# In the sync queue of a convolution and neighbourhood attention kernel, the queries' fill of a chunk goes behind the collecting of denominators and the first maxima, the keys' fill ahead of the spreads

## The reference

```python
x = x + _L0_conv_ref(_gn(x), L0_conv_W)        # 3x3 convolution, 32 groups of 4 channels
x = x + _L1_conv_ref(_gn(x), w_qkv, b_qkv, rpb, w_proj, b_proj)
```

## Time and profile before

| | us |
|---|---|
| median of 3 runs | 1148.31 |
| lowest and highest | 1146.44, 1153.41 |
| the profiled execution | 1146.23 |
| its span, first to last instruction | 1144.3 |
| TensorE (PE) busy | 1023.5 (89%) |
| VectorE (DVE) busy | 800.6 (70%) |
| ScalarE (ACT) busy | 661.2 (58%) |
| GpSimd (POOL) busy | 377.5 (33%) |
| mean granted TensorE clock | 0.916 |

### The profile page before, as it was taken

One profiled execution on the slowest core, in us unless ns is written; L12 is line 12 of the kernel. 1 busy time (PEld: TensorE's weight loads), 2 busy tenths in 40 slices (PEclk: granted clock), 3 DMA queues, 4 the chain that ended last, 5 costly groups with the idle time before them and its releaser, 6 DMA issues.

```text
span 1144.3 us, 41255 instructions
## 1 busy us (share of the span) xinstructions
PE 1023.5 (89%) x16485; PEld 702.3 (61%) x16485; DVE 800.6 (70%) x2159; ACT 661.2 (58%) x1840; POOL 377.5 (33%) x759
## 2 busy tenths in 40 slices
PE   5999999997898989898999898898999898989883
PEld 3666665555566666665666666666666666666661
DVE  3477856336778687776877786868686777777770
ACT  2111312106686767676776768586767776777561
POOL 5000104014252516161534344352525151625230
PEclk9999999998899899988998999899798888998895
DMA  9320014406675757484857676665757584857621
GB/s 248 98 85 30 30 43 124 105 29 175 142 165 131 177 135 188 110 211 98 199 126 197 144 178 139 171 162 136 169 130 183 125 197 102 210 106 178 120 57 58
DMA packets 141525, 154.72 MB, mean 135 GB/s; under 512 B 31344, under 2 KB 119824, under 8 KB 141080
## 3 DMA queue, kind: packets, MB, share of 16 engines
q1 hardware_dynamic: 140344, 148.20, 54.3%
q0 software_dynamic: 992, 3.90, 1.1%
HBM read 84.05 MB, written 67.60 MB: 133 GB/s over the span
## 4 chain that ended last, share of the span: by engine, by line
PE 72%; issue 9%; DMA 7%; DVE 7%; SPq 3%; POOL 1%; ACT 0%; POOLq 0%; DVEq 0%
PE PS L1298 16%; PE PS L1365 14%; PE PS L1402 11%; PE PS L1386 7%; PE PS L1310 6%; PE PS L1379 5%; PE PS L1347 5%; PE PS L1412 4%; DMA area<-q_parts 4%; DVE S L1148 2%; DMA area<-x 2%; PE PS L1327 2%; DVE area L1127 1%; DVE masked L1159 1%; PE PS L1425 1%
## 5 line engine op out<-in xcount | busy, mean ns | idle before, releaser
L690 POOL TENSOR_TENSOR late<-masked 128x48 f32<-128x48 f32 (+1 forms) x512 | 151.5, 296 | 525.2 <-DVE masked L1159 506.0
L1148 DVE TENSOR_TENSOR S<-PS,bias 128x384 f32<-128x384 f32 (+1 forms) x512 | 282.7, 552 | 6.6 <-PE PS L1365 5.1
L1365 PE MATMUL PS<-area 97*128 97x48 bf16 (+1 forms) x4096 | 258.2, 211 | 31.6 <-issue 12.2
L880 ACT ACTIVATE S<-S 128x384 f32<-128x384 f32 (+1 forms) x512 | 272.0, 544 | 9.8 <-DVE S L1148 7.7
L1138 DVE TENSOR_REDUCE mcol<-PS 128x6 bf16<-128x480 f32 (+2 forms) x288 | 176.1, 611 | 127.5 <-PE PS L1386 127.5
L873 ACT ACTIVATE VT<-PS 128x128 f32<-128x128 f32 x448 | 127.8, 285 | 230.3 <-PE PS L1347 229.8
L1365 PEld LDWEIGHTS PS<-area 97*128 97x128 bf16 x4096 | 185.8, 105 | 80.1 <-DVE S L1148 17.5
L1402 PE MATMUL PS<-S,VT 128*18 128x48 f32 x8192 | 203.9, 219 | 28.6 <-issue 24.6
L1402 PEld LDWEIGHTS PS<-S,VT 128*18 128x18 f32 x8192 | 121.3, 101 | 171.4 <-issue 100.4
L1298 PE MATMUL PS<-padded,wconv 128*128 128x392 f32 x576 | 204.4, 503 | 0.0
L1159 DVE TENSOR_TENSOR masked<-PS,cst 128x96 f32<-128x96 f32 (+1 forms) x512 | 128.6, 251 | 65.2 <-PE PS L1402 64.4
(11 more groups left out here) (85 smaller groups left out, 865.0 us busy)
## 6 DMA issues: line engine op xcount, KB each, us to landing
area<-k_parts SPq DMA_DIRECT2D x32, 1008.0 KB, 9.1
area<-q_parts SPq DMA_DIRECT2D x64, 294.0 KB, 10.3
k_parts<-area SPq DMA_DIRECT2D x32, 504.0 KB, 5.9
q_parts<-area SPq DMA_DIRECT2D x64, 196.0 KB, 3.8
k_parts<-area SPq DMA_DIRECT2D x32, 336.0 KB, 5.2
late<-x_mid SPq DMA_DIRECT2D x18, 392.0 KB, 4.8
out<-area SPq DMA_DIRECT2D x18, 392.0 KB
den<-sums SPq DMA_DIRECT2D x132, 49.0 KB
```

Source lines behind the costliest of these rows:

```text
L690: nc.gpsimd.tensor_tensor(sel[:, c % SEL_RING, :, :, t0:t0 + count], m[:, :, 0], m[:, :, 1], ALU.add).then_inc(s["summed"], 1)
L880: nc.scalar.activation(S[:, n % 4, 0:cols], S[:, n % 4, 0:cols], ACT.Exp).then_inc(s["probs"], 1)
L1148: nc.vector.tensor_tensor(S[:, n % 4, 0:cols], PS[:, SCORE + n % 2, 0:cols], bias[:, at:at + cols], ALU.add).then_inc(s["biased"], 1)
L1365: last = mm(PS[:, SCORE + n % 2, cols * g:cols * (g + 1)], key_rows[a][0:PEAK_ROW + 1, g, key:key + 128], query_rows[a][0:PEAK_ROW + 1, g, ...
```

## The change

Two orders in SP's list change, and nothing else; every DMA and every wait is kept.

- Odd loops: the keys' fill of c+1 goes ahead of the spreads of c-1. The queries' fill goes from there to behind the collecting, the first maxima and the packing.
- Even loops: the queries' fill goes from behind the keys' fill to behind the collecting, the keys' store and the first maxima. The packing goes ahead of the queries' store, right behind the queries' fill.

```diff
                 if c % 2:
-                    spread_reciprocals(c - 1)
                     if more:
                         fill_keys(c + 1)
-                        fill_queries(c + 1)
+                    spread_reciprocals(c - 1)
                     collect_denominators(c)
                     if more:
                         move_maxima(c + 1, 0)
                     pack_denominators(c)
+                    if more:
+                        fill_queries(c + 1)
                     if more:
                         move_maxima(c + 1, 1)
                         move_maxima(c + 1, 2)
...
                 else:
                     fill_keys(c + 1)
-                    fill_queries(c + 1)
                     collect_denominators(c)
                     if i + 1 < IMAGES:
                         store_keys(i + 1, 1)
                     move_maxima(c + 1, 0)
+                    fill_queries(c + 1)
+                    pack_denominators(c)
                     if i + 1 < IMAGES:
                         store_queries(i + 1, 0)
-                    pack_denominators(c)
                     if i + 1 < IMAGES:
                         store_keys(i + 1, 2)
                     move_maxima(c + 1, 1)
```

## The result

| | before | after |
|---|---|---|
| median of 4 runs each, us | 1150.86 | 1171.20 |
| lowest and highest | 1146.44, 1157.33 | 1167.28, 1177.43 |
| the profiled execution | 1146.23 | 1167.28 |
| its span | 1144.3 | 1165.3 |

The recorded ratio after to before, of fast runs, is 1.022, with a 95% interval of 1.017 to 1.028 (the medians above give 1.018). The change makes the kernel slower, by 20 us in the medians and 21 us in the profiled executions. The forecast was 1147 us, the range 1131 to 1164 us: the kernel after lies above it.

A forecast was written before the change was run, and what follows sets the result against it. It took gaps at seven even chunk starts, 10.8 us, as the stake, with the maxima landing last. Later landings +5, (d) -2 and slow tiles -2 made together +1 us: 1146.2+1 = 1147 us, range 1131 to 1164.

The forecast's parts named there:

- What bounds the kernel: TensorE's 83 us idle in the stage; gaps at seven even chunk starts, 10.8 us in sum, are the stake.
- (a): Odd loops: keys issued 5.0 us earlier, spreads run behind them; VectorE's division waits 0 to 1 us, taken as 0.
- (b): Odd loops: SP waits for the collected sums behind the spreads; packing goes 5.4 us earlier.
- the backlog: SP's list behind the even loops' maxima: two added issues delay the odd loop by 0 to 1.3 us, taken as 0.5.
- (d): Odd loops: early packing ends VectorE's 16.2 us of waits before the reciprocal; together -2 us.
- (c): Odd loops: queries' fill, issued 6.6 us later, lands 5.3 us after first issue; the expected gain is gone.
- the fourth rival: Waits without a releaser (24.6 and 12.2 us) move with the traffic; widens all ranges by some 3 us; no chance given.
- slow tiles behind a stall: VectorE's part in the slow tiles after a stall goes; minus some 2 us.
- Even loops: Queries' fill, now behind the first maxima, lands before the chunk's scores, with 0.9 us to spare in loop 2.
- The second: Rival: SP's backlog isn't absorbed, query fill slower behind stores; 1.5 us more at nine or ten even starts, 1160 us; chance 0.17.
- The first rival: Even starts become free as collecting and queries land sooner; 1131 us; chance 0.24.

The follow-up runs named there:

- the fastest version: Kernel before with only the odd loops reordered: keys' fill first, queries' fill behind the first maxima and ahead of the packing; median 1113.79 us, ratio 0.972.

## Why the prediction was wrong

**What bounds the kernel**: right in the place (even starts), in that no odd start stalls before, and in that the maxima were last to land; in the kernel after the releaser is the fill itself, as forecast. What it missed is that 39 of the 83 us of idle time were gaps at the instruction packets, which move with the traffic.

**Odd loops (a) and (b)**: right in loop 3. Measured from K = 353.71+5.0: packing was forecast 6.9 us behind K, plus the backlog's 0.5, at 366.1, and goes at 366.22. The wait of VectorE for the packed sums is gone, as (d) said.

**Odd loops (c), the fill's landing: the first step that failed, and the largest term.** I took 5.3 us, with ends implied by 11.6 and 13.5, from the kernel's very first fill. It takes 7.7 us in loop 3 and 7.5 in the mean of the fifteen odd loops. The last landing of loop 3 came at 374.35, K+15.6 on the scale above, where the forecast with its 0.5 us of backlog has K+13.1. What makes it slow stays open: small transfers behind it, the packing close ahead of it, or both (moving it behind the maxima gave 6.2 us in the mean).

**The generalisation from loop 3: the second step that failed.** In loop 3 of the kernel before, SP was later than in any other odd loop: keys 13.4 us behind the first scores of chunk 3, last landing 25.9 us behind them. Over the fifteen odd loops the means are 11.3 and 24.3. Loop 13 is at the other end (the first view below is TensorE's timeline, the second SP's, the third the issue of the maxima with its time to landing):

```profile
615.00 0.30 PE L1365 MATMUL PS<-area 97*128 97x48 bf16 x3
```

```profile
619.83 0.59 SPq L555 DMA_DIRECT2D sums<-packed  x1
622.48 2.64 SPq L566 DMA_DIRECT2D den<-sums  x4
625.22 0.61 SPq L525 DMA_DIRECT2D area<-k_parts  x1
```

```profile
area<-mcol SPq DMA_DIRECT2D x1, 6.0 KB, 8.8
```

Here keys go at +10.2 and the maxima, issued at 629.16, have landed at +23.0, in time. The kernel after, same loop:

```profile
623.53 0.26 PE L1366 MATMUL PS<-area 97*128 97x48 bf16 x2
```

```profile
630.43 0.59 SPq L555 DMA_DIRECT2D sums<-packed  x1
631.12 0.60 SPq L525 DMA_DIRECT2D area<-k_parts  x1
634.61 2.65 SPq L566 DMA_DIRECT2D den<-sums  x4
...
643.25 0.34 SPq L549 DMA_DIRECT2D packed<-sums  x1
643.64 1.41 SPq L516 DMA_DIRECT2D area<-q_parts  x2
```

Keys at +7.6, which is 2.6 us sooner and not the 5.0 that I had from loop 3; the reciprocals are stored at +6.9 instead of +4.8. Packing at +19.7, queries at +20.1, and their landing at +27.6, 0.04 us ahead of TensorE's start at 651.20. So the release moves from +23.0 to +27.6 in loop 13, by 4.6 us, from +25.9 to +28.0 in loop 3, by 2.1 us, and in the mean from +24.3 to +27.6, by 3.3 us. My sum had +0.6 us, and charged it to nine or ten starts instead of fifteen. In the mean, 2.2 us of what was missing are the fill's length (7.5 for 5.3), and 1.0 its later issue: +20.1, where 11.3 and the forecast's 7.8 give +19.1. Had I laid the new order over several loops of the trace instead of one, I'd have seen that the new landing depends on where the reciprocals stand.

**Other idle time: the third step that failed.** It stood in the fourth rival as some 3 us of width, without a sign. The gaps at the instruction packets fell by 36 us, and this both hid and fed the stall: TensorE, no longer held up there, reaches the even start 22.7 us behind the last one's first scores in the mean, before 24.9. So 3.3 us of later landing and 2.2 of earlier arrival, less 0.7 by which TensorE used to come behind the landing, make a mean stall of 4.9 us, and the time grows by far less than the stalls do. The sum as measured, from 258 us to the first scores of chunk 31:

| | forecast, us | measured, us |
|---|---|---|
| gaps at even starts | +5 | +63.2 (10.8 to 74.0) |
| gaps at odd starts | 0 | +2.7 |
| gaps at instruction packets | 0, within 3 | -35.9 (39.1 to 3.2) |
| TensorE's other idle time (forecast: part (d)) | -2 | +1.9 |
| its busy time (forecast: slow tiles behind a stall) | -2 | -11.4 |
| together | +1 | +20.5 |

The third row, which the forecast didn't have, went the other way than the error in the first, and hid over half of it. Why the busy time falls isn't shown.

**Even loops and the backlog**: the fill there lands nearly in time, as forecast (in loop 2 5.7 us after its issue at 340.42, M+7.5 with M = 338.56; the forecast was M+6.6, its late end M+7.9). Odd starts stall by under 1 us. From the first maxima to the storing of reciprocals SP's list takes 15.1 us in loop 12 (615.37 to 630.43) and took 14.5 (605.31 to 619.83): 0.5 us more, as I had. But the chunk start lies nearer to the maxima (8.2 us behind them, before 9.7), because a gap of 1.4 us at an instruction packet (609.11) stood in between and is gone. Against the chunk's start SP is 2.1 us later.

**Rivals.** The second (SP's backlog, 1160 us, chance 0.17) named the right place, and its condition (queries landing after K+13.5) came true. Its cause is real but the smaller part: the even edit alone makes 49.7 us of gaps at even starts, and undoing it leaves 60.0 of the 74.0 us and a loss as large; moving one step of the odd loop removed both. The first rival (even starts become free, 1131 us) is what happens when the packing isn't in front: with the fill one step earlier no even start has a gap, and the time goes beyond that rival's price. The forecast had the wait for the collected sums on the path and placed it rightly in loop 3; it took it as paid for by a short fill. The fourth was real, with 36 us instead of 3, as above.

## What to carry to other kernels

In an ordered DMA list, look at what each step *waits for*, not only at its length: a large transfer with a fixed due time belongs ahead of a step that waits for the landing of earlier small ones. Here one swap of two neighbours was worth 50 us. Lay a new order over several loops of the trace, and not only over the one with the clearest stall. Don't read a sum of waits as time: here 63 us of stalls came and 36 us of other gaps went with the same edit. Look at idle time without a releaser before you leave it out; a gap in the middle of a group of matmuls can't be a wait of the program. And when a change bundles moves, run them apart: keys first alone gains 1.7%, packing before the queries loses more than that.

## What the runs showed of the hardware

- The queries' fill (2 x 294 KB) lands 7.5 us after its first issue in the mean with the packing 0.4 us ahead and the maxima (4.5 and 1.8 KB) right behind, and 6.2 us with the packing 1.7 us and the maxima ahead. Which of the two does it isn't shown.
- TensorE can stall at 16 KB packets of its instruction queue: 21 gaps, 39.1 us in sum, each 256 instructions or a multiple apart, in the kernel before; 3.2 us in the kernel after.
- DMAs with two rows of source move 196 KB at 40 GB/s on a share of 0.13; as eight DMAs of one row each 93 GB/s at 0.39. Eight of these issues take SP as long as four of the others, 2.65 us.
- A 5 us stall is followed by slow work: in the kernel after the granted clock is 0.50, the 1.2 GHz level, from 651.2 to 655.0 us, right behind the gap at chunk 14:

```profile
646.00:651.20 5.20, 0.01 (x2) 0.00 (x0) 1.13 (x5) 2.24 (x8) 0.29 (x1) 0.78 1.09 152
651.20:655.00 3.80, 3.80 (x56) 2.19 (x57) 1.74 (x6) 2.45 (x7) 0.29 (x1) 0.50 0.13 40
```

  Up to the first scores of chunk 31 the lower level takes 164 us in the kernel before and 164 in the kernel after, in which stalls at even starts stand in place of gaps at instruction packets; in the fastest version, which has few of either, it takes 89 us, and the mean clock is 0.94.
